# A two-layer decoder on one core: the last cross-attention streamed from its scores to its output, and experts and gated units written out with the router beside their first products

## The reference, cut to what matters

```python
x = x + _L0_attn_ref(_layernorm(x), ...)           # linear attention
x = x + _L0_xattn_ref(_layernorm(x), ctx, ...)     # 4 layers: self-, cross-attention, MLP
x = x + _L0_ffn_ref(_layernorm(x), ...)            # 8 experts 128->512->128, top-p router
x = x + _L1_attn_ref(_layernorm(x), ...)           # causal attention with decay
x = x + _L1_xattn_ref(_layernorm(x), ctx, ctx, mask, ...)
x = x + _L1_ffn_ref(_layernorm(x), ...)            # 8 gated units 128->192->128 + shared, top-2

# _L1_xattn_ref: 16 heads of 8 channels, 512 queries, 154 keys
Q = query @ Wq.T + bq; K = key @ Wk.T + bk; V = value @ Wv.T + bv
scores = einsum('bhqd,bhkd->bhqk', Q, K) / sqrt(8)
scores = where(mask, -inf, scores)
attn_w = where(isnan(softmax(scores)), 0, softmax(scores))
out = einsum('bhqk,bhkd->bhqd', attn_w, V) ... @ Wo.T + bo

# _L0_ffn_ref: gate = probs * keep (top-p), one column per expert
y = relu(x @ W1[e] + b1[e]) @ W2[e] + b2[e];  out = sum_e gate[e] * y
# _L1_ffn_ref: comb = weights of the two best experts
out = sum_e comb[e] * ((silu(x @ wg[e]) * (x @ wu[e])) @ w_down[e]) + shared
```

## Time and profile before

| | |
|---|---|
| median of 3 runs | 1525.31 us (1519.01 to 1525.95) |
| the profiled execution, its own time | 1523.25 us |
| its span | 1521.2 us |
| mean granted PE clock | 0.927 of full |
| stages of the span, by PE's timeline | start to 60 us, four layers to 1022, router and experts 1034 to 1172, decay attention 1177 to 1213, last cross-attention 1217 to 1406, gated units 1410 to 1517 |

### The profile page before, as it was taken

How to read it: one execution, slowest core, us unless ns; L and a number is a source line. 1 busy time by engine, 2 the same in 40 slices (tenths; PEclk the granted TensorE clock), 3 DMA queues, 4 the chain that set the end, 5 groups by cost and what they waited for, 6 DMA issues and landing times.

```text
span 1521.2 us, 21784 instructions
## 1 busy us (share of the span) xinstructions
PE 1279.8 (84%) x7659; PEld 760.6 (50%) x7666; DVE 716.0 (47%) x2049; ACT 740.8 (49%) x1820; POOL 403.4 (27%) x345
## 2 busy tenths in 40 slices
PE   4599998899998989998989999965997612788688
PEld 2244565454554644555644545544887311333576
DVE  7665644465554455554355564424113561421544
ACT  1276565466666466666547666621443300243332
POOL 0433423443333253332263342211110040000100
PEclk8699999999999999999999999985999855898799
DMA  4000000000000000000000000001110023000010
GB/s 131 0 1 1 22 8 22 12 15 0 22 8 22 8 20 1 22 1 8 22 22 1 1 1 1 1 21 45 29 42 14 0 44 38 3 2 1 9 31 22
DMA packets 29683, 25.55 MB, mean 17 GB/s; under 512 B 4506, under 2 KB 23575, under 8 KB 29591
## 3 DMA queue, kind: packets, MB, share of 16 engines
q1 hardware_dynamic: 29591, 24.33, 6.3%
HBM read 22.71 MB, written 1.61 MB: 16 GB/s over the span
## 4 chain that ended last, share of the span: by engine, by line
PE 76%; DVE 11%; DMA 3%; POOL 3%; issue 3%; ACT 2%; SPq 1%; another core or an unknown queue 0%; DVEq 0%; ACTq 0%; POOLq 0%
PE bank L1487 12%; PE bank L1446 9%; PE bank L1465 8%; PE bank L1506 6%; PE bank L1518 6%; PE bank L1498 4%; PE bank L1695 4%; PE bank L1462 4%; PE bank L1439 3%; PE bank L1511 2%; PE bank L1601 2%; PE bank L1603 2%; PE bank L1602 2%; PE bank L1868 2%; DMA QA<-dram_q 2%
## 5 line engine op out<-in xcount | busy, mean ns | idle before, releaser
L833 DVE CUSTOM_DVE_ANT_0 bank<-bank,maskrow 128x512 f32<-128x512 f32 x256 | 172.4, 716 | 151.5 <-PE bank L1446 151.4
L1215 ACT ACTIVATE probs<-bank,tops 128x512 f32<-128x512 f32 x256 | 174.3, 685 | 128.1 <-DVE tops L833 128.0
L646 POOL TENSOR_TENSOR rot<-rot,sin 128x512 f32<-128x512 f32 (+1 forms) x112 | 134.2, 1199 | 376.3 <-DVE rot L822 376.3
L1227 ACT ACTIVATE KA<-bank 128x512 f32<-128x512 f32 x256 | 139.2, 601 | 31.8 <-PE bank L1465 31.8
L1446 PE MATMUL bank<-QA 64*128 64x512 f32 x512 | 146.7, 653 | 7.6 <-DVE rot L822 7.0
L1465 PEld LDWEIGHTS bank<-ident,probs 128*128 128x128 f32 x1024 | 116.8, 141 | 54.4 <-issue 45.5
L1465 PE MATMUL bank<-ident,probs 128*128 128x128 f32 x1024 | 134.7, 274 | 2.3 <-ACT Vs L1194 2.3
L1487 PE MATMUL bank<-KA,Vs 128*64 128x512 f32 x512 | 135.4, 615 | 0.0
L648 POOL TENSOR_TENSOR QA<-rot 128x512 f32<-128x512 f32 x96 | 121.7, 1268 | 7.5
L1211 ACT ACTIVATE probs<-bank,tops 128x154 f32<-128x154 f32 x256 | 95.5, 383 | 57.2 <-DVE tops L830 56.6
L821 DVE TENSOR_TENSOR rot<-bank,cos 128x512 f32<-128x512 f32 (+1 forms) x112 | 73.9, 660 | 74.3 <-PE bank L1506 55.5
(11 more groups left out here) (252 smaller groups left out, 2288.7 us busy)
## 6 DMA issues: line engine op xcount, KB each, us to landing
f<-in_fW SPq DMA_DIRECT2D x8, 256.0 KB, 3.1
Vc<-in_wup SPq DMA_DIRECT2D x8, 192.0 KB, 2.4
QA<-dram_q SPq DMA_DIRECT2D x6, 256.0 KB
wk<-in_sWk SPq DMA_DIRECT2D x4, 256.0 KB, 2.8
wq<-in_sWq SPq DMA_DIRECT2D x4, 256.0 KB, 3.3
wv<-in_sWv SPq DMA_DIRECT2D x4, 256.0 KB, 4.7
wo<-in_sWo SPq DMA_DIRECT2D x4, 256.0 KB, 2.8
ck<-in_cWk SPq DMA_DIRECT2D x4, 256.0 KB, 2.6
```

Of the source, the lines that this page charges most:

```text
L646: g.tensor_tensor(turned, turned, tab, ALU.mult).then_inc(q.pool_step, 1)
L833: v.tensor_tensor_reduce(bank[i][:, :], bank[i][:, :], maskrow[:, u.b * S:(u.b + 1) * S], -SCALE, 3.0e38, ALU.add, ALU.min, tops[:, g % 4, ...
L1215: c.activation(to, bank[i][:, :], ACT.Exp, bias=tops[:, g % 4, e, 0:1], scale=-1.0, accum_out=sums[:, n, k, e:e + 1]).then_inc(q.probs_rea ...
L1227: c.activation(turned_self(u)[:, half, :, k * P:(k + 1) * P], bank[4 + half][:, :].rearrange("p (c t) -> p c t", t=P), ACT.Copy).then_inc( ...
```

## The change

1. Start: the turns of the mask (L1610 ff.) and the copy to `maskT` are gone.
2. Experts: the hardware loops and the drains are gone; all eight experts (and eight gated units and the shared one) are written out. The first expert's weights are loaded during the last layer and split before the inputs are there; the inputs are rounded and completed for each half apart. PE's first instructions behind the inputs are the up-products of expert 0 for the first half, then the router, then those for the second half. Gates are turned and the biases computed during expert 1. ACT takes the router's exponential between the two halves' ReLUs. For the gated units the same, with the ranking on DVE cut into pieces that stand between the products of unit 0 (`route1`), and the exponential behind the SiLUs of both halves.
3. Last cross-attention: keys and queries stay float32 on chip. DVE makes four copies of the keys in `KZ`, each with the rows of other heads zeroed (`last_keys`), between the two norm parts ahead of the decay attention; the values go into `Vx` behind it (`last_values`). 32 steps follow, each for 128 queries and four heads: mask product and 32-row score product into two banks, DVE's negated maximum of each bank, four exponentials of 154 columns with that maximum as bias, four turns of the first 128 keys into bank 4 or 5 and one turn of the four heads' last 26 keys, which POOL has copied next to each other into `xpad`. DVE takes the main turn out, ACT the tail (once in two steps). Each eighth of the work (4 steps' worth) is then weighed: `weigh_main` and `weigh_tail`, four products each of 32 output columns, then `heads_turn`, `divide`.
4. No transfer takes part in the last cross-attention any more. `Vx`, `xpad` are cleared by POOL during the decay attention instead of the three memsets.

The core of the diff:

```diff
             pe.wait_ge(q.ctx_in, see.next(q.ctx_in, 16))
...
-            pe.wait_ge(q.mask_ready, see.next(q.mask_ready))
-            for k in range(2):
-                for t in range(TB):
-                    c0 = k * (S // 2) + t * P // 2
-                    ins = turn(bank[3][:, c0:c0 + P // 2].bitcast(BF16), maskq[:, t, k * C2:k * C2 + P], identb[:, :])
...
-            inputs()
-            router(wr[:, 0, :], True)
-            pe.wait_ge(q.gate_ready, see.next(q.gate_ready))
...
-            with pe.Fori(0, E // 2) as i:
...
-                drain()
+            inputs()
+            for e in range(E):
+                for b in range(B):
+                    expert_up(e, b)
+                    if e == 0 and b == 0:
+                        router(wr[:, 0, :], True)
+                if e == 1:
+                    gates_turn()
+                for b in range(B):
+                    expert_down(e, b)
+                if e == 1:
+                    expert_biases()
...
+            def last_scores(hs):
+                n, b, ii, t, half = xstep(hs)
...
+                for gg in range(2):
+                    i = 2 * half + gg
+                    free(i)
+                    mm(bank[i][:, 0:2 * C].rearrange("p (a c) -> p a c", a=2), identb[:, :],
+                       maskq[:, t, :].unsqueeze(1).broadcast_to([P, 2, C]), start=True, stop=False)
+                for gg in range(2):
+                    i = 2 * half + gg
+                    r = slice(32 * i, 32 * i + 32)
+                    mm(bank[i][:, 0:2 * C].rearrange("p (a c) -> p a c", a=2), QX[r, b * S + t * P:b * S + (t + 1) * P],
+                       KZ[r, b, 2 * ii:2 * ii + 2, :], start=False, stop=True).then_inc(q.xs_full, 1)
...
+            def last_turns(hs):
+                i = 4 + hs % 2
+                pe.wait_ge(q.xp_ready, hs + 1)
+                free(i)
+                for j in range(4):
+                    ins = turn(bank[i][:, j * P:(j + 1) * P], XP[:, hs % 4, j, 0:P], ident[:, :])
+                ins.then_inc(q.xmain_full, 1)
+                lend([i], q.xmain_out)
+                pe.wait_ge(q.xpad_ready, hs + 1)
...
+            for hs in range(2):
+                last_scores(hs)
+            for hs in range(XSTEPS):
+                last_turns(hs)
+                if hs + 2 < XSTEPS:
+                    last_scores(hs + 2)
+                n, k = hs // 8 - 1, hs % 8
+                if n >= 0 and k % 4 == 0:
+                    weigh_main(n, k // 4, 7)
+                if n >= 0 and k % 4 == 1:
+                    weigh_tail(n, k // 4, 7)
+                if n >= 0 and k % 4 == 3:
+                    heads_turn(n, k // 4, 7)
```

DVE's and POOL's parts of a step, and DVE's ranking for the gated units:

```diff
+                for hs in range(XSTEPS):
+                    main_out(hs)
+                    if hs + 2 < XSTEPS:
+                        maximum(hs + 2)
+                    if hs >= 8 and hs % 8 == 3:
+                        divide(hs // 8 - 1, 0, bank[7])
...
+                for hs in range(XSTEPS):
+                    pool.wait_ge(q.xp_ready, hs + 1)
+                    if hs >= 2:
+                        pool.wait_ge(q.xtail_full, hs - 1)
+                    g.tensor_copy(xpad[:, hs % 2, :, 0:C2], XP[:, hs % 4, :, P:C]).then_inc(q.xpad_ready, 1)
...
-                rank(logits)
-                softmax_of(logits)
+                softmax_of(logits)
+                beaten_by(logits)
+                glu_products(0)
+                beaten_count()
+                glu_products(1)
```

More of the change, by code:

```diff
@@ L31 @@
 H1, DK = 16, 8
-SPLITS = 6
 SCALE = DH ** -0.5
@@ L154, with inputs_before @@
 ORDER = Order()
+def inputs_before():
+    layers = B + sum(p.what == "turn" for step in ORDER.steps for p in step.pieces)
+    return dict(moe=layers, glu=layers + 3 * B)
+INPUTS = inputs_before()
 def biases(l):
@@ L188, in expect @@
         return self.n[sem.name]
[L190 to L203 removed]
+    next = expect
 def decoder(nc, a, out):
@@ L313, in decoder @@
         row = KT[:, 2, 512:512 + TILES]
-        rcx = KA[:, 6656:6672]
+        row16 = [KT[:, 2, 528 + 16 * i:544 + 16 * i] for i in range(2)]
         w1a = cq[:, :].rearrange("p (a n) -> p a n", a=4)
@@ new lines, in _, with gates_of_glu @@
+            gathered(0, bank[0])
+            heads_out(3, 0, bank[1])
+            heads_out(3, 1, bank[3])
+            gathered(1, bank[6])
+            g2 = slice(0, 2 * HALF)
+            act.wait_ge(q.w_glu0, 32)
+            split_weights(wh[0][:, g2], gup[0][:, g2])
+            halved_inputs()
+            def gates_of_glu(b):
+                for k in range(2):
+                    act.wait_ge(q.glu_gate_full, see.next(q.glu_gate_full))
+                    c.activation(GS[:, b, k, :], bank[2 * k][0:HP, :], ACT.Silu).then_inc(q.glu_act, 1)
@@ L1704, in _ @@
+            lend([0], q.xk_ready)
             inputs()
@@ new lines, in heads_turn, with gather @@
+            def heads_turn(n, half, i):
+                pe.wait_ge(q.xo_ready, 2 * n + half + 1)
+                free(i)
+                for t in range(TB):
+                    ins = turn(bank[i][:, t * P:(t + 1) * P], O4[half][:, t * P:(t + 1) * P], ident[:, :])
+                ins.then_inc(q.xt_full, 1)
+                lend([i], q.xn_ready)
+            def gather(b, i):
+                pe.wait_ge(q.xn_ready, 4 * b + 4)
+                free(i)
+                for t in range(TB):
+                    ins = turn(bank[i][:, t * P:(t + 1) * P], OX[:, b, t, :], ident[:, :])
+                ins.then_inc(q.xg_full, 1)
+                lend([i], q.xoT_ready)
@@ L1873, in _ @@
-            drain()
-            pe.wait_ge(q.split_ready, see.next(q.split_ready))
-            with pe.Fori(0, E // 2) as i:
-                see.enter(i, EXPERTS1)
-                for k in range(2):
-                    w = (q.w_glu0, q.w_glu1)[k]
-                    pe.wait_ge(w, see.next(w, 32))
-                    glu(k, gdn[k])
-                drain()
-                see.leave(E // 2)
-            glu(2, gdn[2])
+                    glu_up(e, n, b)
+                    if e == 0 and b == 0:
+                        router(wr[:, 1, :], False)
```

864 lines of the change are left out of this document (387 added, 477 removed).

## The result

The changed kernel takes 1397.68 us (median of four runs, 1397.06 to 1397.99), the kernel before 1525.63 us beside it: ratio 0.917, 95% interval 0.916 to 0.919. The forecast was 1404.

What follows compares the result with a forecast made beforehand. PE, busy 84% of the span, was taken as the bound, with gains where it idles or its clock is low. Terms -2.2, -23.1, +2.5, -80.9 and -15.2 sum to -118.9, from 1523.25 to 1404 us; range 1385 to 1441.

Steps and rivals of the forecast that it cites:

- Start, -2.2: Kernel start: PE's mask turns and the wait ahead of them both go, saving 2.2 us, or 0 if weights are late.
- Experts, -23.1: Experts: earlier first up-product, no waits at loop ends, router at full clock; end at 1148.5 instead of 1171.6, saving 23.1 us.
- Keys, values, memsets, +2.5: Ahead of the decay attention: `last_keys` adds 2.0 us and the new memsets 0.5, together 2.5 us more.
- the fear behind the 0.5: Norm beside the new POOL memsets: they may hold DVE's scalings up, taken as 0.5 us, bounds 0 and 1.5.
- Last cross-attention, -80.9: Last cross-attention: 32 steps of 2.5 us plus an end of 17.5, x complete at 1324.8 instead of 1405.7, saving 80.9 us.
- for the hand-overs that PE can't fill I take 2.5 us per step: Last cross-attention's steps: PE's own 2.3 us raised to 2.5 for hand-overs, 80 us in all, bounds 2.1 and 3.3.
- Gated units, -15.2: Gated units: first up-product 6.5 us behind x instead of 19.2, unit 0 takes 16, eight others 74; saving 15.2 us.
- PE better than its sum: Rival: last cross-attention's steps take 2.1 us each and the experts are at their best, 1389 us; chance 0.13.
- The ring: Rival: last cross-attention's round over PE, DVE, ACT and POOL sets the pace, 3.3 us per step, 1430 us; chance 0.2.
- slower: Rival: POOL's tail copy in each step of the last cross-attention takes 7 us, 1548 us in all; chance 0.02.
- Half clock: Rival: PE's waits within the last cross-attention's steps drop the clock, 2.3 becomes 4.6 us per step, 1471 us; chance 0.05.
- the old pairs: Old kernel's paired products on 64 rows, 1.06 us against 0.97 for one: at most 0.1 for both mode changes, so nothing added.

Runs made afterwards that it cites:

- combined: Changed kernel with the last cross-attention's end reordered, router tiles spread between up-products, one-row bias products removed and the context loaded right behind x: 1380.8 us, ratio 0.906.
- router_ahead: Changed kernel with the experts' router, gate turns and biases again ahead of the first expert product, without loops or drains: 1408.8 us, ratio 0.925.
- experts_as_before: router_ahead, with PE also waiting after each second expert and each second gated unit until every bank is read: 1421.6 us, ratio 0.933.
- memset_back: Changed kernel plus one POOL memset of 8,192 columns beside DVE's scaling ahead of the last cross-attention: 1403.0 us, ratio 0.921.
- pool_more: Changed kernel with POOL copying 1,024 unread columns ahead of each tail copy in the last cross-attention's steps: 1414.7 us, ratio 0.927.
- one_ahead: Changed kernel with the last cross-attention's scores, maxima and exponentials one step ahead instead of two: 1474.4 us, ratio 0.969.
- no_mask: Changed kernel without the two mask products in each step of the last cross-attention, so masked keys are counted: 1409.9 us, ratio 0.922.
- same_rows: Changed kernel with both score products of a step on the same 32 array rows, so half of the heads get wrong scores: 1440.2 us, ratio 0.944.
- no_mask_filled: no_mask plus 14 turns that nobody reads in PE's wait ahead of the first step of the last cross-attention: 1390.5 us, ratio 0.913.

## Why the prediction was right, and where it wasn't

*Start, -2.2: 0.8 where it can be read.* The step said that both the mask's turns and their wait go. They do, but the context's transfer, issued at the same time as before (5.7), lands at 12.49 where it landed at 10.74, and its turns wait for it.

```profile
10.74 0.75 PE L1610 MATMUL bank<-ident,probs 77*128 77x77 f32 x4 [10.74 <-DMA probs<-in_ctx]
```

```profile
12.49 0.75 PE L1578 MATMUL bank<-ident,probs 77*128 77x77 f32 x4 [12.49 <-DMA probs<-in_ctx]
```

The first line is of the kernel before. 0.8 of the 2.2 are left at the first products (14.97 against 15.75). The -0.2 at the experts' turns is within the layers' spread and shows neither a gain nor its loss; nor does combined, with 1.7 us at the start. Why the transfer lands later is open.

*Experts, -23.1: right in mechanism (router_ahead, experts_as_before), 3.5 too much.* The terms mis-sized are the router and the clock. I halved the router's 8.1 at half clock to 4.1 at full, but its products of eight columns go from 0.52 only to 0.32, so it has 5.0 at full, and with the clock's fall it took 6.4. For the low clock I gave 1.5; the 24 up-products around the router took 9.1 where 5.5 is full clock, 3.6 more. The first product (1037.6 for 1038.1), the gate turns and biases (2.8) and the units without idle time between them came as worked out; all the rest together was 0.9 better. That PE has no wait between the experts is in the trace; which part of it the loops' branches are was not tried.

*Keys, values, memsets, +2.5: +2.2.* Here `last_keys` took 2.11 for 2.0, and the memsets nothing for 0.5. memset_back shows that the fear behind the 0.5 had a cause: a long memset beside a norm's scalings holds them up for nearly its length (6.5 of 6.94).

*Last cross-attention, -80.9: right side, 11.5 too little.* The step that failed is "for the hand-overs that PE can't fill I take 2.5 us per step". PE's sum of 2.3 was exact (2.28), and nothing had to be added: with two steps on the ring of 3.57, each has 1.79 for itself, less than PE's 2.28. Where PE is the slower the hand-overs hide, where it isn't (eight steps) the step is 1.79 and not 2.5; and the last two steps have no scores to compute. The 32 steps took 66.8 for 80, and 1.2 of the gain stand ahead of them. Against that the end took 20.5 for 17.5: the wait of 2.95 behind the first half's statistics was not in the sum, and the last projection ran at half clock (5.8 for 3.4).

*Gated units, -15.2: -16.2, right.* First up-product 6.2 us behind x (6.5), unit 0 16.2 (16), the others 9.15 (9.2).

*The rivals.* "PE better than its sum" came nearest in the steps, by its own price of 2.1 per step (66.8 / 32 = 2.09); by the total, 1397.7 lies between its 1389 and the forecast's 1404, because 3.5 of the experts and 3.0 of the end went the other way. That the forecast is within 7 us is partly luck: an error of 13 in the steps met these. "The ring" and "slower" had the right path and the wrong length: waits met within the steps only in pool_more. "Half clock" got 0.05 and deserved more: four small edits (one_ahead, no_mask, same_rows, pool_more) brought it about. The change waits 0.74 us at the place where no_mask waits 1.81, and keeps its clock. The argument against it, waits of 0.3 that kept 0.93, looked at the old steps and not at the wait ahead of the first new one.

*Rule and trace.* The Trainium skill, page "TensorEngine Tiling (Array Packing)", section "Key Properties", has each change of mode drain PE, and the prediction added nothing for it. In the steps nothing is to be seen beyond the start distances. But no_mask shows 0.09 more from a full-row turn to the 32-row scores than to a full-row product, and the one-row products 0.4 us per tile (router: 0.63 with, 0.21 without). If the one-row product of the router itself takes the 0.21 of its neighbour, 0.2 are left for the two changes around it, 0.1 each, which agrees with the 0.09. By that the trace would side with the rule on the fact, and the old pairs hid it. In the steps it stands inside start distances that the sum had taken whole. That these 0.1 are drains is argued, not shown.

## What to carry to other kernels

An allowance for hand-overs is added to a step only where the ring, divided by the steps on it, is longer than the busiest engine's work; otherwise the engine's own sum is the step. Where the work differs from step to step, count it step by step and not by the mean (pool_more). Ahead of a loop with a lean PE, look at the wait ahead of its first step: filled with products that nobody reads it can be worth far more than it is long (19 us for 1.75, without the masks; it was not tried in the change, whose clock holds). And a bias by a one-row product of ones is dear: added by the engine that reads the bank anyway, or ahead of time to the residual, it frees PE and, in both places here, the clock came back: some 6 us in the experts' start and 7.5 in the end of the last cross-attention.

## What was not expected of the hardware

- The granted clock falls while PE is busy without a gap: at 1045.1 in the router of the change, and for 66 us of 66 busy in same_rows (0.53). It stayed at half for 45 us in no_mask with PE busy 16.00 of 16 us. So busy time alone, as the trace counts it, does not bring it back, and what does stays open. (Ends of PE instructions are modelled, so "busy" says that one record follows the other.) The Trainium skill, page "TensorE: Matmul & The Clock Gate", Part 1, lets the clock follow how busy PE has been; if busy means that an instruction runs, these rows disagree.
- One edit of 1.75 us of unread turns changed the time by 19 us. Once down, the clock outlived the wait by 45 us in the profiled execution of no_mask.
- POOL's copies of 1,024 columns left DVE's passes from PSUM as they were (0.69), while a memset held DVE's scaling between SBUF tiles back for 6.5 of 6.94 us and 1 us of short ones did not.
- The layers' length differs by up to 2.7 us between profiled executions with the same instructions up to there (the experts' turns come between 1033.5, in pool_more, and 1036.3, in no_mask_filled), more than several terms of the sum. It stays open why.
